# Expert weights as the stationary side in the second tile mixture of a four-layer kernel

## The reference, cut to what matters

```
x = hidden_states.reshape(-1, D)                      # D = 256, E = 8, K = 2, H = 512
scores = softmax(x @ gate_w.T)
top_scores, sel = top_k(scores, K)
x_sorted = x[tok_sorted]                              # rows grouped by expert
h = silu(ragged_dot(x_sorted, w1, gs)) * ragged_dot(x_sorted, w3, gs)
y = ragged_dot(h, w2, gs)
out[tok_sorted] += y * scores_sorted[:, None]
```

## Time and profile before

| | |
|---|---|
| median of 3 runs | 2252.8 us (2248.62 to 2253.13) |
| the profiled execution, its own time | 2270.9 us |
| its span, first to last instruction | 2269.1 us |
| TensorE busy in it | 2003.8 us, 88% |
| VectorE, ScalarE, GpSimd busy | 1111.9, 988.4, 559.8 us |
| the stage of `f3` | from 2005.7 to 2244 us of the span |

### The profile page before, as it was taken

How to read it: one execution, slowest core, us unless ns; L and a number is a source line. 1 busy time by engine, 2 the same in 40 slices (tenths; PEclk the granted TensorE clock), 3 DMA queues, 4 the chain that set the end, 5 groups by cost and what they waited for, 6 DMA issues and landing times. The chain is left out here.

```text
span 2269.1 us, 44780 instructions
## 1 busy us (share of the span) xinstructions
PE 2003.8 (88%) x15891; PEld 1420.8 (63%) x15891; DVE 1111.9 (49%) x3378; ACT 988.4 (44%) x2602; POOL 559.8 (25%) x872
## 2 busy tenths in 40 slices
PE   6899999988999998799967856996889999969994
PEld 3477777744677776466654645884567777736663
DVE  5388882274888824100034445107578883431113
ACT  2388881145888822111112331223578883212221
POOL 2022210066111105311115343115711111421111
PEclk9999999988999999899978985998989999979997
DMA  2185523000644221433122552641010004131113
GB/s 85 43 239 147 157 81 98 0 1 22 169 113 114 58 75 40 139 110 103 62 78 74 161 171 76 210 137 42 0 51 21 21 12 150 47 124 45 47 43 122
DMA packets 158555, 197.81 MB, mean 87 GB/s; under 512 B 15443, under 2 KB 132142, under 8 KB 158348
## 3 DMA queue, kind: packets, MB, share of 16 engines
q1 hardware_dynamic: 146732, 168.83, 24.7%
q0 software_dynamic: 11616, 26.26, 3.2%
HBM read 120.33 MB, written 88.64 MB: 92 GB/s over the span
## 5 line engine op out<-in xcount | busy, mean ns | idle before, releaser
L995 ACT ACTIVATE att_pr<-all_h,att_nmax 128x128 f32<-128x128 f32 (+3 forms) x768 | 420.9, 551 | 53.7 <-DVE att_nmax L948 53.7
L1059 PEld LDWEIGHTS att_t_ps<-all_ident,att_pr 64*128 64x128 f32 x3840 | 163.7, 139 | 104.7 <-issue 48.5
L1255 PE MATMUL out_y_ps<-outw_wo,mem_qt 128*128 128x256 f32 x768 | 181.5, 391 | 0.0
L1059 PE MATMUL att_t_ps<-all_ident,att_pr 64*128 64x64 f32 x3840 | 170.3, 224 | 10.5 <-DVE att_pt L957 10.4
L1929 PE MATMUL exp_f_h_ps<-exp_f_xs_t,cw_f_w 128*128 128x512 f32 (+1 forms) x512 | 173.3, 498 | 1.5 <-DVE exp_f_xs_t L1967 1.5
L1941 PE MATMUL exp_f_y_ps<-cw_f_w,exp_f_hid 128*128 128x256 f32 x768 | 168.4, 379 | 0.0
L957 DVE COPY att_pt<-att_t_ps 128x1024 f32<-128x1024 f32 (+2 forms) x168 | 166.6, 991 | 0.0
L1255 PEld LDWEIGHTS out_y_ps<-outw_wo,mem_qt 128*128 128x128 f32 x768 | 146.7, 196 | 25.6 <-issue 6.2
L1997 ACT ACTIVATE exp_f_hid<-exp_f_h_ps 128x512 f32<-128x512 f32 (+1 forms) x128 | 62.4, 490 | 219.9 <-PE exp_f_h_ps L1929 217.0
L1941 PEld LDWEIGHTS exp_f_y_ps<-cw_f_w,exp_f_hid 128*128 128x128 f32 x768 | 144.8, 190 | 19.5 <-issue 0.5
L948 DVE CUSTOM_DVE_ANT_0 all_h<-att_s_ps,att_bias,mem3k_nsn 128x128 f32<-128x128 f32 (+3 forms) x256 | 128.3, 549 | 37.0 <-PE att_s_ps L1042 27.6
(11 more groups left out here) (395 smaller groups left out, 3666.7 us busy)
## 6 DMA issues: line engine op xcount, KB each, us to landing
sorted_c<-all_zero SPq DMA_DIRECT2D x8, 2056.0 KB, 13.5
sorted_f<-all_zero SPq DMA_DIRECT2D x8, 2056.0 KB, 11.6
cw_f_w<-in_L_ffn_w_dram SPq DMA_DIRECT2D x16, 1024.0 KB, 8.0
cw_f_w<-in_L_ffn_W_dram SPq DMA_DIRECT2D x12, 1024.0 KB
band<-rev SPq DMA_DIRECT2D x2, 4096.0 KB, 18.8
att_bias<-band SPq DMA_DIRECT2D x32, 256.0 KB, 3.1
com_f_rows<-expert_f SPq DMA_DIRECT2D x16, 512.0 KB, 6.4
tw_f_wab<-in_L_ffn_w_dram SPq DMA_DIRECT2D x2, 4096.0 KB, 19.9
```

The source lines that it names most:

```text
L995: nc.scalar.activation(pr[u % 4][:, hh, at], sc[u % 4][:, hh, at], ACT.Exp, scale=-1.0, bias=nmax[:, b + k, q, h:h + 1], accum_out=rsum[:, ...
L1059: last = nc.tensor.transpose(t_ps[e % 2][:, half, (q + 1) * (n * hh + k) + kb, :], pr[u % 4][d, hh, at:at + P], c.ident[d, d])
L1255: nc.tensor.matmul(y_ps[b % 2][:, q, :], c.out_t[:, p, P * at:P * (at + 1)], wo[:, p, :], start=(p == 0), stop=False)
```

## The change

In `f3` (nothing of it acts in `c2`, where `small` is true), the weights become the stationary side of the first products, in pieces of 128 columns, and the turned rows the moving side, 128 columns. So there are 16 products of 128 columns in the place of 4 of 512, and the result has the hidden column as the partition and the token along it, which is the form that the second product wants as stationary: the turns of `hid` and ScalarE's copies of them are gone, and the second product runs one tile behind, not two. The expert's weights are copied per tile from `tw.wab` to one of two fixed buffers `now`, one half (128x1024) by GpSimd, ahead of the scatter in its order, the other by VectorE, behind the product of `hid`; both read the expert's number into a register, as TensorE still does for the second product. The ring of rows has 3 buffers and not 4, the ring of results 2 and not 4, silu's result and `hid` are one buffer.

```diff
-        self.G, self.r = 4, r
+        self.G, self.r = 4 if first_tile is None else 3, r
...
-    GY = 6 if small else G
-    GI = 2 * GY if small else G
+    GY = 6 if small else 2
+    GI = 2 * GY
+    LAG = 2 if small else 1
...
-        act = [m.sb(f"act{n}", [P, F]) for n in range(2)]
...
-        hid_t = [m.sb(f"hid_t{n}", [P, FC, P]) for n in range(2)]
+        act = [m.sb(f"act{n}", [P, F]) for n in range(2)] if small else hid
+        if small:
+            hid_t = [m.sb(f"hid_t{n}", [P, FC, P]) for n in range(2)]
+        else:
+            now = [m.sb(f"now{n}", [P, KD, 2, F]) for n in range(2)]
...
+            def take_weights(t):
+                expert = pool.value_load(r.owner[0:1, t:t + 1], min_val=0, max_val=E - 1)
+                if t >= 2:
+                    pool.wait_ge(ab_ready, t - 1)
+                pool.tensor_copy(weights_now(t, 0), kept_weights(expert, 0)).then_inc(now_0, 1)
+
+            if not small:
+                pool.wait_ge(tw.loaded, 32)
+                take_weights(0)
+                take_weights(1)
             for t in range(N):
+                if not small and t + 2 < N:
+                    take_weights(t + 2)
                 pool.wait_ge(y_copied, t + 1)
...
+                    pe.wait_ge(now_0, t + 1)
+                    pe.wait_ge(now_1, t + 1)
                     for n in range(2):
-                        for k in range(KD):
-                            last = nc.tensor.matmul(ab_ps[t % 2][:, n, :], xs_t[t % (AHEAD + 1)][:, k, :], tw.wab[:].rearrange("p (e k) n f -> p k n e f", k=KD)[:, k, n, at, :].rearrange("p a f -> p (a f)"),
-                                                    start=(k == 0), stop=(k == KD - 1))
+                        for f in range(FC):
+                            for k in range(KD):
+                                last = nc.tensor.matmul(ab_ps[t % 2][:, n, P * f:P * (f + 1)], now[t % 2][:, k, n, P * f:P * (f + 1)], xs_t[t % (AHEAD + 1)][:, k, :],
+                                                        start=(k == 0), stop=(k == KD - 1))
...
-                pe.wait_ge(ht_copied, t + 1)
+                if small:
+                    pe.wait_ge(ht_copied, t + 1)
+                else:
+                    pe.wait_ge(hid_ready, t + 1)
...
-                if t >= 2:
-                    last_product(t - 2, expert.pop(t - 2))
-                if 1 <= t <= N:
+                if t >= LAG:
+                    last_product(t - LAG, expert.pop(t - LAG))
+                if small and 1 <= t <= N:
                     turn_hidden(t - 1)
...
+            def take_weights(t):
+                expert = dve.value_load(r.owner[0:1, t:t + 1], min_val=0, max_val=E - 1)
+                if t >= 2:
+                    dve.wait_ge(ab_ready, t - 1)
+                nc.vector.tensor_copy(weights_now(t, 1), kept_weights(expert, 1)).then_inc(now_1, 1)
+
+            if not small:
+                dve.wait_ge(tw.loaded, 32)
+                take_weights(0)
             for t in range(AHEAD):
                 take_x(t)
                 if small:
                     take_idx(t)
+            if not small:
+                take_weights(1)
             for t in range(N + 1):
...
                     nc.vector.tensor_tensor(hid[t % 2][:], (lin if mx.gate else act)[t % 2][:], ab_ps[t % 2][:, 1, :], ALU.mult).then_inc(hid_ready, 1)
+                if not small and t + 2 < N:
+                    take_weights(t + 2)
```

More of the change, by code:

```diff
@@ L2057, in experts_by_tile @@
         x_ps = [m.ps(f"x_ps{n}", [P, KD, P]) for n in range(AHEAD)]
-        t_ps = m.ps("t_ps", [P, FC, P])
+        if small:
+            t_ps = m.ps("t_ps", [P, FC, P])
         y_ps = [m.ps(f"y_ps{n}", [P, D]) for n in range(2)]
         stored, stored_0 = zip(*(m.pool_dma_sem(f"stored{n}", len(range(n, N, GY))) for n in range(GY)))
-        names = "xt_ready xt_copied ab_ready act_ready lin_ready hid_ready ht_ready ht_copied y_ready y_copied idx_copied".split()
-        (xt_ready, xt_copied, ab_ready, act_ready, lin_ready, hid_ready, ht_ready, ht_copied, y_ready, y_copied, idx_copied) = (m.sem(x) for x in names)
+        names = "xt_ready xt_copied ab_ready act_ready lin_ready hid_ready ht_ready ht_copied y_ready y_copied idx_copied now_0 now_1".split()
+        (xt_ready, xt_copied, ab_ready, act_ready, lin_ready, hid_ready, ht_ready, ht_copied, y_ready, y_copied, idx_copied, now_0, now_1) = (m.sem(x) for x in names)
         block = stack.enter_context(nc.Block())
@@ L2086, in _, with kept_weights, weights_now @@
             com.sync(sp)
+        def kept_weights(expert, k):
+            return tw.wab[:].rearrange("p (e k) n f -> p k e n f", k=KD)[:, k, ds(expert, 1), :, :].rearrange("p a n f -> p (a n f)")
+        def weights_now(t, k):
+            return now[t % 2][:, k, :, :].rearrange("p n f -> p (n f)")
         @block.gpsimd
         def _(pool):
+            def take_weights(t):
[7 more added lines that the diff above has]
+                take_weights(1)
             for t in range(N):
+                if not small and t + 2 < N:
+                    take_weights(t + 2)
                 pool.wait_ge(y_copied, t + 1)
@@ L2136, in last_product @@
                 for f in range(FC):
-                    last = nc.tensor.matmul(y_ps[t % 2][:], hid_t[t % 2][:, f, :], tw.wd[:].rearrange("p (e k) f -> p k e f", k=FC)[:, f, ds(expert, 1), :].rearrange("p a f -> p (a f)"),
+                    last = nc.tensor.matmul(y_ps[t % 2][:], hid_t[t % 2][:, f, :] if small else hid[t % 2][:, P * f:P * (f + 1)], tw.wd[:].rearrange("p (e k) f -> p k e f", k=FC)[:, f, ds(expert, 1), :].rearrange("p a f -> p (a f)"),
                                             start=(f == 0), stop=(f == FC - 1))
@@ L2144, in _ @@
             expert = {}
-            for t in range(N + 2):
+            for t in range(N + LAG):
                 if t < N:
@@ L2161, in _ @@
                     if t >= 2:
-                        a.wait_ge(lin_ready if mx.gate else hid_ready, t - 1)
+                        a.wait_ge(lin_ready if mx.gate else y_ready, t - 1)
                     nc.scalar.activation(act[t % 2][:], ab_ps[t % 2][:, 0, :], ACT.Copy if mx.gate else ACT.Silu).then_inc(act_ready, 1)
-                if 1 <= t <= N:
+                if small and 1 <= t <= N:
                     a.wait_ge(ht_ready, t)
@@ L2168, in _ @@
                     nc.scalar.activation(hid_t[(t - 1) % 2][:], t_ps[:], ACT.Copy).then_inc(ht_copied, 1)
-                if t >= 2:
-                    v = t - 2
+                if t >= LAG:
+                    v = t - LAG
                     a.wait_ge(y_ready, v + 1)
@@ L2209, in _ @@
                     if t >= 2:
-                        dve.wait_ge(ht_ready, t - 1)
+                        dve.wait_ge(ht_ready if small else y_ready, t - 1)
                     nc.vector.tensor_tensor(hid[t % 2][:], (lin if mx.gate else act)[t % 2][:], ab_ps[t % 2][:, 1, :], ALU.mult).then_inc(hid_ready, 1)
+                if not small and t + 2 < N:
+                    take_weights(t + 2)
 class Combine:
```

## The result

The changed kernel takes 2243.46 us in the median (18 runs, 2238.04 to 2250.2), the kernel before on the same chips 2250.86 (18 runs). The ratio is 0.9966, 95% interval 0.9957 to 0.9975: 7.7 us faster (the two medians lie 7.4 apart). The forecast was 12.3 us (0.9945), its range 2235 to 2248.

A forecast was written before the change was run, and what follows sets the result against it. TensorE was taken to bound the steady stretch, 5.82 us per tile falling to 5.44. The pace gave -14.0 us, the clock +1.7, other head and tail terms cancelled: 2252.8 - 12.3 = 2240.5 us, range 2235 to 2248.

The forecast's parts named there:

- the signs of being wrong: First products waiting for the copied weights, a pace of the 32 records above 0.115 us, or loads of rows waited for.
- The term of the record: First products: 32 records of 128 columns at 0.109 us each, 3.49 us per tile, 0.05 more than before.
- the 144-column row: Profile row of products with 144 moving columns, taken as the upper bound for a short record: 0.121 us.
- the 8-column row: Profile row of the router's 16 products with 8 moving columns, taken as the lower bound for a short record: 0.106 us.
- The rival priced at p = 8.03: First products: weight loads of 0.19 us don't overlap at all, 8.03 us per tile, 2336 us in all; chance 0.02.
- The wait for `tw.wd` and the clock: Stage head: TensorE idles some 3.5 us for the second matrix, then the lower clock costs 1.7 us, bounds 0 and 3.4.
- the rival of the costlier head (-9.5): Stage head: `tw.wd` lands no earlier (+1.1) and the clock stays low for two stretches (+1.7), 2243.3 us; chance 0.12.
- GpSimd's order: GpSimd's scatter, weights, scatter: slack 1.3 us, no cost. Rival that it bounds the kernel: +4.7 us, 2257.5; chance 0.08.
- x: GpSimd's register read, weights copy and any hold-up: forecast 1.82 us, costing from 3.13, worse than before from 3.79.
- VectorE's copy: VectorE's 128x1024 weights copy, priced at 1.22 us as from PSUM; made two tiles ahead, so nothing waits for it.
- The rings: Buffers of rows and of results, cut to 3 and 2 from 4 each: forecast to cost nothing.
- The rule of load and product pairs: Skill page's rule for first products: 0.158 us per record, 7.0 us per tile, +45 us, 2298 us.

## Why the prediction was right, and by how much it was off

The mechanisms were right, and the gain came out at 0.63 of its size. That 2243.46 us lies only 3 from the forecast of 2240.5 is in part luck: the forecast stood on the three runs shown, 2252.8, and the 18 runs of before have their median 1.9 lower. By the forecast's own signs the pace (0.1117, forecast 0.106 to 0.11), the wait (4.5 us, forecast 3 to 4) and the last second product (7 us sooner, forecast 12) were missed, and of the signs of being wrong one showed, once: the first tile's products waited 2.1 us for GpSimd's copy into `now`. They started 1.5 us later after the first transpose than before, where the forecast had 1.2 for VectorE, and as it said the wait for `tw.wd` hides that.

- *TensorE bounds the steady stretch before and after*: right, 201.10 of 201.10 us.
- *The turns of `hid` go, 0.43 us per tile, and the pace falls with the columns*: right as a mechanism. The term of the record was mis-sized: 0.1117 us, not 0.109. The 0.109 came from transposes (0.43/4 is 0.1075; their starts lie 0.109 apart in the trace), whose weight loads take 0.14 us against 0.19 of a product. The right row was there and I read it badly. For the 144-column row I took the length less the last load over 15 steps, for the 8-column row the distance to the next line's load over 16. Read the first way the latter gives (1.86 - 0.19)/15 = 0.111, the measured value. It was the product bound by its load, and so no bound from below but the answer: at 128 columns the load, 0.1117, is longer than the columns' 0.109, and the experiment with 64 columns shows it. That is 37 x 0.08 = 2.9 us of the gain. The rival priced at p = 8.03 was no test of loads that don't overlap the product: it counts the load alone, and load plus product would be 0.30 a record. In the steady stretch the load does overlap it.
- *The wait for `tw.wd` and the clock*: the place was right, the size too small. `tw.wd` came at 17.75 us after the first transpose, forecast 16.77: SP issued it 1.1 us sooner as expected, but it took 1.0 longer (+1.0 us), which the forecast put at nothing; the instructions loaded inside the transfer are the likely reason. So TensorE stood idle for 4.5 us and not 3.5, and the clock was at half for 6.8 us, twice the stretch of the earlier trace rows. 226.58 - 17.75 - 37 x 5.518 - 1.51 = 3.2 us, where 1.7 was the value and 3.4 the bound (+1.5 us). Work in the wait gave 2.9 of it back.
- *The sum*: -12.3 + 2.9 + 1.0 + 1.5 = -6.9; the stage shows -7.0, the runs -7.7. It is the rival of the costlier head (-9.5) with the pace on top, and stays under half a per cent for these two reasons.
- *GpSimd's order*: the cover held. Reading the register cost nothing there (the copy at 2067.59 follows the scatter at once), and a copy took 1.05 us, forecast 1.02. So x was 1.05, not 1.82, and four copies moved the time by the forecast's sum. The hold-up is real, in both directions, but lay elsewhere: VectorE's copy takes 0.69 us alone and 1.26 at the head and up to 2.06 with four copies on GpSimd beside it, and GpSimd's second copy at the head took 1.50 beside it, 1.05 otherwise. In the steady stretch VectorE's copy ends (2065.58) before the scatter starts (2066.61), and nothing is held up. The Trainium skill's rule ("SBUF — State Buffer", in "Who interferes with whom", on the shared port pair, which one engine holds for its whole instruction) agrees in direction with these rows; that such a copy keeps a scatter from its descriptors, they don't show.
- *VectorE's copy* was priced by the row from PSUM, 1.22 us; it takes 0.69. Hidden either way.
- *The rings*: right, nothing.
- *The rule of load and product pairs* ("TensorE: Matmul & The Clock Gate" in the Trainium skill, 81 ns against 56): the trace doesn't agree for fp32. 0.1117 against 0.109 is 1.02, not 1.45. Its direction, that the load sets the pace at short columns, is what the runs show.
- *The profiled execution 18.1 us above the median*: not carried over. The changed kernel's took 2240.3 us, 3.2 under its median. By the second trace of before, the surplus lay ahead of the stage (first transpose at 2005.78 against 1989.22).
- *The tail*: right; the last two second products follow one another (16 records from 2206.78 on, in 3.65 us).

## What to carry to other kernels

An fp32 product with a short moving side costs its weight load, here from 128 columns down: before cutting products into shorter ones, read the pace of a stream of short ones from starts, the same way for every row, and compare it with the columns' own. Bringing a consumer closer to its producer shortens the tail but also moves the first consumer forward, here into a transfer that wasn't there yet; the idle time costs itself and then the clock, so keep the distance of the first one and put ready work into the wait. Price the head of a stage apart from its steady stretch, and measure inside the stage, since whole executions differ by more than such a change. And look for packets of instructions inside a transfer that is waited for: the kernel with the short products loads 229 of them in all, the one before 220.

## What was not expected of the hardware

Within a stream, a record of a 128x128 fp32 weight load and its product took 0.1117 us with 128 moving columns and with 64; a 64-column record whose load was done took 0.056. Idle stretches of TensorE of 4.5 and 5.8 us each brought 6.8 us at half the granted clock, one of 0.6 us none; the 3.4 us of the earlier trace rows had brought 3.4. The clock fell 0.8 and 1.9 us before the two long ones ended. VectorE's copy of 128x1024 in SBUF took 0.69 us and up to 2.06 beside copies on GpSimd. The 4 MB transfer took 14.4 and 14.5 us in the kernel before and 15.4 to 15.8 in all with the new stage, where a 16 KB load of instructions lay inside it.
